# A graph network on one core: softplus's last step from DVE to POOL, and the clearing ahead of the messages' wait

## The reference, cut to what matters

```python
signal = jax.nn.softplus(_batchnorm(z @ W_core.T + b_core, gamma_core, beta_core))
gate = jax.nn.sigmoid(_batchnorm(z @ W_filter.T + b_filter, gamma_filter, beta_filter))
message = gate * signal
nbr_sumed = jax.ops.segment_sum(message, dst, num_segments=atom_features.shape[0])
```

## Time and profile before

| what | value |
|---|---|
| median of 3 runs | 14080.94 us (14061.56 to 14081.86) |
| the profiled execution | 14056.44 us, span 14053.5 us |
| PE busy | 6581.5 us, 47% of the span |
| DVE busy | 6540.1 us, 47% |
| ACT busy | 1956.0 us, 14% |
| POOL busy | 8844.8 us, 63% |
| L1530, softplus on DVE | 208 times, 254.6 us |

### The profile page before, as it was taken

The page is one execution under the profiler, slowest core; times in us unless marked ns, Lnnn a source line. Parts: engine busy times, 40 slices in busy tenths (PEclk is TensorE's granted clock), DMA queues, the critical chain, the costliest instruction groups (busy, mean ns, idle before and its releaser), DMA issues.

```text
span 14053.5 us, 162350 instructions
## 1 busy us (share of the span) xinstructions
PE 6581.5 (47%) x40047; PEld 5632.1 (40%) x40048; DVE 6540.1 (47%) x13266; ACT 1956.0 (14%) x3268; POOL 8844.8 (63%) x8158
## 2 busy tenths in 40 slices
PE   5777777774555555788500000284333334333334
PEld 4777777774555555677400000173111112111112
DVE  5444444444666666899500000397434344434344
ACT  1111111111222222566300000000000001000000
POOL 2888888884777777100377777402777773777773
PEclk7666666666777777899655555697555555555555
DMA  4333333333444444333122222232111111111111
GB/s 96 18 18 18 18 18 18 18 18 62 126 126 127 126 126 127 107 98 99 50 54 54 54 54 55 61 97 63 39 39 39 39 39 33 39 39 39 39 39 26
DMA packets 851569, 827.49 MB, mean 59 GB/s; under 512 B 630205, under 2 KB 636579, under 8 KB 848948
## 3 DMA queue, kind: packets, MB, share of 16 engines
q0 software_dynamic: 450064, 387.16, 18.7%
q1 hardware_dynamic: 398252, 436.72, 9.9%
q10 hardware_dynamic: 3218, 3.20, 0.1%
HBM read 571.32 MB, written 255.06 MB: 59 GB/s over the span
## 4 chain that ended last, share of the span: by engine, by line
POOL 51%; issue 22%; PE 11%; DMA 8%; DVE 5%; SPq 1%; DVEq 1%; POOLq 0%; ACT 0%; ACTq 0%
POOL tab L728 21%; POOL aux L702 10%; POOL lane_tab L685 10%; DMA lane_tab<-rows,idx 7%; POOL buf_b L702 6%; POOL acc_w L702 4%; PE ps L1089 3%; PE ps L1200 1%; PE ps L979 1%; PE ps L1136 1%; PE ps L1122 1%; DVE buf_b L1658 1%; SPq L552 1%; POOL t_first_tab L713 1%; PE ps L963 1%
## 5 line engine op out<-in xcount | busy, mean ns | idle before, releaser
L728 POOL DMA_INDIRECT tab<-gcn_tab,idx x3136 | 2984.0, 952 | 1826.1 <-issue 1825.2
L685 POOL DMA_INDIRECT lane_tab<-rows,idx x1664 | 2597.7, 1561 | 661.8 <-issue 659.0
L1101 PE MATMUL ps<-ident_b,zero_b 128*128 128x512 bf16 x1664 | 773.2, 619 | 2917.7 <-issue 1551.2
L1737 DVE TENSOR_REDUCE buf_d<-ps 128x512 f32<-128x1536 f32 x416 | 731.1, 1757 | 2299.8 <-PE ps L1105 2299.8
L702 POOL DMA_INDIRECT aux<-att_tab,idx x1568 | 1486.9, 948 | 477.7 <-issue 477.7
L1101 PEld LDWEIGHTS ps<-ident_b,zero_b 128*128 128x128 bf16 x1664 | 182.0, 128 | 3282.1 <-issue 1788.3
L702 POOL DMA_INDIRECT buf_b<-src_tab,idx x832 | 838.3, 1008 | 414.1 <-issue 253.4
L1003 PE MATMUL ps<-ident,srcg 128*128 128x128 f32 x3328 | 695.2, 393 | 727.1 <-DVE srcg L1356 727.1
L702 POOL DMA_INDIRECT acc_w<-src_tab,idx x832 | 815.6, 980 | 253.6 <-issue 247.2
L1003 PEld LDWEIGHTS ps<-ident,srcg 128*128 128x128 f32 x3328 | 643.8, 297 | 772.7 <-DVE srcg L1356 772.5
L1179 PE MATMUL ps<-ident,acc_w 128*128 128x128 f32 x13 | 3.0, 422 | 1954.5 <-ACT idx L819 1954.5
(11 more groups left out here) (297 smaller groups left out, 14373.0 us busy)
## 6 DMA issues: line engine op xcount, KB each, us to landing
y_stash<-buf_c SPq DMA_DIRECT2D x208, 512.0 KB, 2.8
tab<-y_stash SPq DMA_DIRECT2D x208, 512.0 KB, 3.3
aux<-in_edge_attr_dram SPq DMA_DIRECT2D x1696, 32.0 KB
h_stash<-aux SPq DMA_DIRECT2D x196, 264.0 KB, 2.0
tab<-gcn_tab,idx POOLq DMA_INDIRECT x3136
buf_c<-h_stash SPq DMA_DIRECT2D x156, 264.0 KB, 2.7
lane_tab<-rows,idx POOLq DMA_INDIRECT x1664, 3.2
aux<-att_tab,idx POOLq DMA_INDIRECT x1568
```

Source lines behind the costliest of these rows:

```text
L685: pool.indirect_dma_start(lane_tab[k][:, :], bass.IndirectOffsetOnAxis(ap=idx[:, b, u:u + 1], axis=0), rows[:, b, u, 0:D1], None, compute_ ...
L728: pool.indirect_dma_start(g_rows[k][:, u, :], None, table[:, :], bass.IndirectOffsetOnAxis(ap=idx[:, k % RING, u:u + 1], axis=0)).then_inc ...
L1101: pe.matmul(ps[:, 4 * (q % 2) + c, :].rearrange("p (k f) -> p k f", f=P), zero_b[:, :], bc(ident_b[:, :].unsqueeze(1), [P, 4, P]), start=T ...
L1737: dve.tensor_reduce(g_sum[b], parts(4 * b), AX.X, ALU.add).then_inc(s.split_joined, 1)
```

## The change

Softplus's last step leaves DVE. POOL gets a loop over all 208 groups, between the gathers of the first pass and the scatters: for each group it waits for ACT's Abs and rectifies z in place, then waits for ACT's Ln (and its own rectifying) and adds the logarithm. `l1b_softplus` counts two for each group, and its waits on ACT and PE are set to that. On PE, `add_group` is written into `lb_sums`, and the clearing and the load of the offsets stand ahead of the waits for one-hot and messages, behind the wait for the previous addition.

```diff
--- before.py
+++ after.py
@@ -705,6 +705,18 @@
             pool.wait_ge(s.tab_stored, CHUNKS * 16)
             gathers(src_tab, l1_rows, s.l1_indices, s.l1_rows_used)
 
+            with pool.Fori(0, TURNS) as i:
+                for k in range(RING):
+                    t = i * RING + k
+                    z = z_buf[:, k, :]
+                    pool.wait_ge(s.l1b_act, t * 3 + 1)
+                    pool.sem_inc(s.passed, 1)
+                    pool.tensor_relu(z, z).then_inc(s.l1b_softplus, 1)
+                    pool.wait_ge(s.l1b_act, t * 3 + 3)
+                    pool.sem_inc(s.passed, 1)
+                    pool.wait_ge(s.l1b_softplus, t * 2 + 1)
+                    pool.tensor_add(z, z, log_buf[:, k % 2, :]).then_inc(s.l1b_softplus, 1)
+
             pool.wait_ge(s.tpos_clean, 16)
             pool.wait_ge(s.t_places, 1)
             for c in range(CHUNKS):
@@ -848,7 +860,7 @@
                     a = log_buf[:, k % 2, :]
                     act.wait_ge(s.l1b_normed, t + 1)
                     if age >= 2:
-                        act.wait_ge(s.l1b_softplus, t - 1)
+                        act.wait_ge(s.l1b_softplus, t * 2 - 2)
                     act.activation(a, z_buf[:, k, :], ACT.Abs).then_inc(s.l1b_act, 1)
                     act.wait_ge(s.l1b_act, t * 3 + 1)
                     act.activation(a, a, ACT.Exp, scale=-1.0).then_inc(s.l1b_act, 1)
@@ -1078,18 +1090,6 @@
 
             pe.wait_ge(s.bn_ready, 1)
 
-            def add_group(left, right, g, bank, n):
-
-
-                for c in range(2):
-                    pe.matmul(ps[:, bank + c, :].rearrange("p (k f) -> p k f", f=P)[:, :, 0:n], zero_b[:, :],
-                              bc(ident_b[:, 0:n].unsqueeze(1), [P, 4, n]), start=True, stop=False, skip_group_check=True)
-                rel = load8(mybir.EngineType.PE, rel_s, g, (G - 1) * P)
-                for u in range(G):
-                    last = pe.matmul(ps_flat[:, bass.ds(rel[u] + bank * 512, n)], left[:, u, :], right[:, u, 0:n],
-                                     start=False, stop=True, skip_group_check=True)
-                return last
-
             def aggregate(left_ready, conv, free, done):
                 def group(i, q, landed):
                     g = i * RING + q
@@ -1123,13 +1123,20 @@
                 last.then_inc(s.l1b_turned, 1)
 
             def lb_sums(g, q):
+                pe.wait_ge(s.l1b_added, g + 1)
+                for c in range(2):
+                    pe.matmul(ps[:, 6 + c, :].rearrange("p (k f) -> p k f", f=P)[:, :, 0:D1], zero_b[:, :],
+                              bc(ident_b[:, 0:D1].unsqueeze(1), [P, 4, D1]), start=True, stop=False, skip_group_check=True)
+                rel = load8(mybir.EngineType.PE, rel_s, g, (G - 1) * P)
                 pe.wait_ge(s.l1b_hot, g + 1)
                 pe.wait_ge(s.l1b_messages, g + 1)
-                pe.wait_ge(s.l1b_added, g + 1)
-                add_group(lb_hot[q], lb_rows[q % 2], g, 6, D1).then_inc(s.l1b_sums, 1)
+                for u in range(G):
+                    last = pe.matmul(ps_flat[:, bass.ds(rel[u] + 6 * 512, D1)], lb_hot[q][:, u, :], lb_rows[q % 2][:, u, 0:D1],
+                                     start=False, stop=True, skip_group_check=True)
+                last.then_inc(s.l1b_sums, 1)
 
             def lb_back(g, q, age):
-                pe.wait_ge(s.l1b_softplus, g + 1)
+                pe.wait_ge(s.l1b_softplus, g * 2 + 2)
                 if age >= 1:
                     pe.wait_ge(s.l1b_messages, g)
                 for u in range(G):
@@ -1523,11 +1530,6 @@
                     if age >= 4:
                         dve.wait_ge(s.l1b_sums, t - 3)
                     one_hot(dve, lb_hot[k], t).then_inc(s.l1b_hot, 1)
-                if 1 <= age <= 2 * ITER:
-                    z = z_buf[:, (k - 1) % 4, :]
-                    dve.wait_ge(s.l1b_act, t * 3)
-                    dve.wait_ge(s.l1b_normed, t)
-                    dve.scalar_tensor_tensor(z, z, 0.0, log_buf[:, (k - 1) % 2, :], ALU.max, ALU.add).then_inc(s.l1b_softplus, 1)
                 if age >= 3:
                     w0 = load1(mybir.EngineType.DVE, win_s, t - 3, W - 1)
                     dve.wait_ge(s.l1b_sums, t - 2)
```

## The result

The changed kernel takes 14,227.5 us (median of 6 runs, 14,193.7 to 14,279.3) against 14,071.3 us of the kernel before (6 runs, 14,031.8 to 14,119.4): ratio 1.013 as it was measured and recorded, 95% interval 1.010 to 1.016 (the quotient of the two medians shown is 1.011). It is slower by 1.1 to 1.3%; the forecast was 13,919 us, faster by 1.1%, and the range ended at 14,110.

A forecast was written before the change was run, and what follows sets the result against it. The loop PE, ACT, DVE, PE was taken to bound the second pass; 4.41 us plus 0.12 for slow steps gives 4.53 in place of 5.31, 162 us off 14,080.9, so 13,919 us; range 13,875 to 14,110.

The forecast's parts named there:

- The bound of the kernel before: Edge network's second pass: the loop PE, ACT, DVE, PE sets the pace, 5.23 us a step at full clock.
- DVE's own 4.97 us: DVE's work per step in the second pass without waiting, taken as the second bound close behind the loop.
- clearing ahead alone, put at 54 us: Case where only PE's early clearing counts and DVE's pace binds: 54 us gained, 14,027; chance 0.25 shared with another rival.
- Part 1: Clearing and offsets load on PE go ahead of the wait for messages: loop falls from 5.23 to 4.41 us.
- The argument for the lower end: First-pass products follow a similar load without a gap, so PE's load bubble may be covered: 4.33 rather than 4.49 us.
- The addition for slow steps: Steps at the lower clock hurt more as PE has less slack: 0.12 us a step in place of 0.08.
- the path without POOL: Second-pass step set by the loop, with slow steps included: 4.53 us in place of 5.31.
- Part 3: POOL's rectifying (1.4 us) and addition (2.2 us) per step, 3.8 us with hand-over, stay covered by the 4.41 us loop.
- R + A: POOL's rectifying plus addition time per step: middle 3.6 us, binding only above 4.2 without sharing.
- Rival A: DVE's one-hot and POOL's reading exclude each other: 65 us off, 14,016; chance 0.25 shared with another rival.
- B: POOL is the bound through the same exclusion: 5.83 us a step, 108 us more, 14,189; chance 0.18.
- The sign named for A or B: One-hot L444 or idle before it grows to 2 us and more, or POOL busy without gaps while PE waits.

The follow-up runs named there:

- e1: Changed kernel without POOL's loop, softplus's last step back on DVE, clearing and offsets load still ahead; 4.75 us a step, ratio 0.992 to the kernel before.
- e8: Kernel before with softplus as log(1 + exp(z)), no Abs or last step, clearing ahead as in the change; 4.45 us a step, ratio 0.985.
- e4: Changed kernel with the rectifying on ACT, POOL only adding; 4.48 us a step, ratio 0.986 to the kernel before.
- e3: Changed kernel, but DVE's one-hot reads its second input from PSUM, so has one SBUF input; 5.20 us a step, ratio 0.999 to the kernel before.
- e2: Changed kernel with clearing and load back behind the waits, POOL's softplus step kept; 5.33 us a step, ratio 0.999 to the kernel before.
- e7: Kernel before plus one POOL filling a step of a tile nobody uses; 5.31 us a step, ratio 1.000.
- e6: Kernel before plus one POOL rectifying a step of a tile nobody uses; 5.32 us a step, ratio 0.998.
- e9: Changed kernel with DVE's one-hot behind the addition of windows, waiting for the turning back; 5.3, then 6.8 us a step, ratio 0.999 to the kernel before.
- e12: Kernel with POOL's softplus step but no clearing ahead, one-hot made ahead of the normalization; 5.97 us a step, ratio 1.009 to the kernel before.
- e5: Changed kernel with POOL's rectifying replaced by adding a tile of zeros; 5.69 us a step, ratio 1.005 to the kernel before.

## Why the prediction was wrong

**The bound of the kernel before** was named rightly: e1 shows that taking the clearing out of the loop shortens a step at once. *DVE's own 4.97 us* was too much by 0.22: I read it from distances between starts, and two of them, the 1.26 us from L444 to L1530 and the 0.70 left of the way from L1508 to the messages, held 0.11 and 0.09 us of idling that the list of waits does not show. e1's DVE, busy all the time, measured 4.75. Hence the decomposition failed as well: clearing ahead alone, put at 54 us, gave 106 in the medians and 117 by the step.

**Part 1** (4.33 to 4.49 us, taken 4.41) was right: 4.45 in e8 and 4.48 in e4. The argument for the lower end failed; no load was in the way, but the handing over of the messages is longer than to the clearing. *The addition for slow steps* had the wrong sign: I put 0.12 us for 0.08, and the granted clock went to 1.00 in e1, e4 and e8, the slow steps vanished. The two errors partly cancel, and 4.53 us for the path without POOL was 0.05 to 0.08 too long.

**Part 3 is the step that failed.** The addition was sized well, 2.36 us for 2.2; the Trainium skill's figure (GPSIMD Engine Reference, Performance versus the Vector engine), an estimate of 2.25 us here, was as near: the trace agrees with it within 0.11 us. The rectifying took 2.77 us for my 1.4, and 0.97 us more than my high end of 1.8: I bounded it by streams read and written at the rate of a filling, and this instruction is not limited by its streams: the addition reads one more and takes 0.41 us less. That alone puts POOL's own sum at 5.20 us (e3), above 4.41, and eats the whole gain: e3 and e2 lie at the kernel before, within 0.2%. The sentence that POOL "binds only above R + A = 4.2 and even at 4.5 gives 4.7 us, still faster" held an end that was no end: R + A is 5.13.

**Rival A and B** had the right mechanism. The exclusion, which the forecast's own sum put at nothing, added 0.94 us on top (e3), and that is the loss. The Trainium skill's rule (SBUF — State Buffer, Who interferes with whom) agrees for POOL's addition, which the one-hot waits out whole (3.39 us in the change's timeline), and e7 doesn't speak against it for filling, which only writes. For the rectifying it differs: the one-hot waits for the first 0.92 us and not for the whole instruction (e6), and the measurement decides. B's sum of 5.83 us and 14,189 us came close to 6.15 and 14,227, by terms that were 1.8 + 2.7 where the chip has 2.77 + 2.36. It was given 0.18, because I took the middle of two bounds of which the upper was no bound. What no rival had is that the exclusion is a matter of place: it costs 0.94 us in the change and next to nothing in e2, with the same instructions, since the rectifying holds DVE off for 0.92 us only. In e2 the one-hot is held 0.15 us at a time and POOL's instructions average 2.78 and 2.37 us, as in e3; the 0.12 us by which its step is longer is POOL idle, part of it in waits for ACT's Abs (12.9 us in 800). The two parts of the change, each harmless or good (1.00 and 0.99), are bad together (1.01). That the earlier message time is what moved the one-hot into the addition is argued from the timelines of e2 and the change (it starts 0.75 us into the rectifying there, 1.27 us into the addition here); shown is that moving the one-hot alone makes either kernel fast or slow (e9, e12).

**What would show it.** The sign named for A or B, L444 at 2 us and more or POOL without gaps, is what the rows have: L444 up to 3.40 us, 2.07 on average, and POOL busy 197 of 200.

## What to carry to other kernels

Before moving work to an engine whose instruction the trace doesn't have, measure that one instruction; a bound made of other instructions' rates is an estimate; here the value taken from it, 1.4 us, was half of the 2.77 that the instruction took, and the upper bound of 1.8 was passed by 0.97. When a two-input elementwise instruction goes to POOL, look for DVE instructions with two SBUF inputs and ask where in the period each falls: the same pair cost 0.94 us or next to nothing, and a place that works may be narrow. And of a change in two parts, try each alone: here one half by itself gave 0.8% and the other nothing, and together they lost 1.3%.

## What the runs showed of the hardware

- POOL's rectifying of 128x1024 fp32 takes 2.77 us, its addition of two such tiles 2.36 us, its filling 0.95 us (e3, e5, e7). The rectifying, with one input, takes longer than the addition, with two.
- The addition holds off a one-hot with two SBUF inputs to its end: the one-hot ends 1.08 us behind it, after up to 3.40 us (the change). The rectifying does so for about its first 0.92 us, not longer (e6); why, no run shows.
- POOL's instructions wait in turn for a one-hot that has begun: 3.7 us in place of 2.77 for the rectifying, 3.3 in place of 2.37 for the addition (the change).
- One-hots with one input in PSUM take 1.22 us beside POOL's additions and aren't held off (e3).
- Two activations on ACT that don't wait for each other start 0.95 to 0.96 us apart, Abs and the Exp that waits for it 1.08 (e4).
- A pass with this exclusion had two rhythms, 5.3 and 6.8 us a step on average, and changed over within one execution (e9).
